# A fused attention and expert kernel: another order on the DMA-issuing engine, and the first expert block's loads and first product moved ahead

## The reference, cut to what matters

```python
def reference(x, ctx, ...):        # x: (2, 1024, 256), ctx: (2, 154, 256)
    x = x + xattn(layernorm(x), ctx, Wq, bq, Wkv, bkv, Wo, bo)
    return x + ffn(layernorm(x), Wg, bg, W1, b1, W2, b2)
# xattn: 16 heads of 16, scores * 1/4 - slope[h] * |k - q - (Nk - Nq)|, softmax over 154 keys,
#        weighted values, output product
# ffn:   gate = softmax(x @ Wg + bg) over 8 experts; the best two, weights made to sum to 1;
#        out = sum over e of (gelu(x @ W1[e] + b1[e]) @ W2[e] + b2[e]) * weight[e]
#        W1[e]: (256, 1024), W2[e]: (1024, 256)
```

## Time and profile before

| | us |
|---|---|
| median of 3 runs | 430.56 |
| lowest, highest | 430.1, 745.77 |
| profiled execution, its time | 427.04 |
| profiled execution, its span | 425.1 |
| PE busy in the span | 383.0 (90%) |
| DVE, ACT, POOL busy | 317.0, 217.8, 186.3 |
| mean granted clock of PE | 0.971 of full |

### The profile page before, as it was taken

One profiled execution on the slowest core, in us unless ns is written; L12 is line 12 of the kernel. 1 busy time (PEld: TensorE's weight loads), 2 busy tenths in 40 slices (PEclk: granted clock), 3 DMA queues, 4 the chain that ended last, 5 costly groups with the idle time before them and its releaser, 6 DMA issues.

```text
span 425.1 us, 15171 instructions
## 1 busy us (share of the span) xinstructions
PE 383.0 (90%) x4834; PEld 300.9 (71%) x4834; DVE 317.0 (75%) x989; ACT 217.8 (51%) x587; POOL 186.3 (44%) x273
## 2 busy tenths in 40 slices
PE   4669999997988999889999999999999999999960
PEld 3547777765766778677777777776778777777740
DVE  6476999997987888834789789776687777777760
ACT  2345778875766766635474344444443444444420
POOL 3300268885766666444454223333133333333341
PEclk9996999999999999969999999999999999999995
DMA  7659768676677964165234553333432333333210
GB/s 277 134 117 277 215 198 239 208 226 206 212 221 215 277 199 149 53 158 156 64 40 84 111 90 47 53 50 47 54 44 39 46 45 46 45 53 47 28 15 0
DMA packets 73441, 50.88 MB, mean 120 GB/s; under 512 B 48400, under 2 KB 67472, under 8 KB 73232
## 3 DMA queue, kind: packets, MB, share of 16 engines
q1 hardware_dynamic: 66168, 41.44, 36.6%
q0 software_dynamic: 7152, 8.47, 12.0%
q10 hardware_dynamic: 48, 0.01, 0.0%
HBM read 28.52 MB, written 17.37 MB: 108 GB/s over the span
## 4 chain that ended last, share of the span: by engine, by line
PE 45%; DMA 2%; DVE 2%; issue 2%; POOL 1%; ACT 1%; ACTq 0%; POOLq 0%; DVEq 0%
PE ps L1256 44%; DMA out<-stage,row_id 2%; DVE area L1171 1%; DVE area L1169 0%; ACT area L800 0%; POOL out L620 0%; POOL xlist L596 0%; ACT L810 0%; DVE st L966 0%; PE ps L1394 0%; DVE stage L1200 0%; DVE stage L1197 0%; DVE xn L847 0%; ACTq L800 0%; DVE stage L1204 0%
## 5 line engine op out<-in xcount | busy, mean ns | idle before, releaser
L1256 PEld LDWEIGHTS ps<-stage,wts 128*128 x1872 | 130.8, 98 | 40.1 <-issue 1.6
L1256 PE MATMUL ps<-stage,wts 128*128 128x128 f16 x1872 | 155.0, 219 | 1.0 <-issue 1.0
L1256 PE MATMUL ps<-wts,area 128*128 x624 | 150.3, 327 | 0.0
L800 ACT ACTIVATE area<-ps,late 128x128 f32<-128x128 f32 x312 | 89.0, 369 | 114.4 <-PE ps L1256 114.4
L620 POOL DMA_INDIRECT out<-stage,row_id x39 | 68.5, 1755 | 130.2 <-DMA out<-stage,row_id 77.2
L1256 PE MATMUL ps<-area 128*128 128x128 f16 (+5 forms) x784 | 63.1, 230 | 10.1 <-DMA area<-qd 7.6
L1169 DVE TENSOR_SCALAR area<-area 128x512 f16<-128x512 f32 x78 | 33.9, 435 | 41.9 <-ACT area L800 39.9
L1256 PEld LDWEIGHTS ps<-area 128*128 128x128 f16 (+1 forms) x784 | 47.4, 104 | 21.6 <-issue 7.5
L917 DVE TENSOR_REDUCE mx<-ps 128x3 f32<-128x462 f32 (+1 forms) x96 | 53.2, 575 | 9.9 <-PE ps L1256 9.8
L1171 DVE SCALAR_TENSOR_TENSOR area<-area 128x512 f16<-128x512 f32 x78 | 54.8, 703 | 2.7
L663 ACT ACTIVATE area<-ps 128x512 f32<-128x512 f32 x80 | 46.5, 600 | 11.7 <-PE ps L1256 11.6
(11 more groups left out here) (131 smaller groups left out, 414.9 us busy)
## 6 DMA issues: line engine op xcount, KB each, us to landing
stage<-in_w SPq DMA_DIRECT2D x32, 512.0 KB, 4.4
area<-qd SPq DMA_DIRECT2D x16, 256.0 KB, 3.7
qd<-wts SPq DMA_DIRECT2D x48, 64.0 KB, 2.1
area<-in_x SPq DMA_DIRECT2D x16, 128.0 KB, 3.3
out<-area SPq DMA_DIRECT2D x16, 128.0 KB
xlist<-pad_rows SPq DMA_DIRECT2D x15, 130.0 KB, 3.5
area<-nbT SPq DMA_DIRECT2D x64, 1.0 KB
area<-in_b SPq DMA_DIRECT2D x1, 1024.0 KB, 5.8
```

Source lines behind the costliest of these rows:

```text
L800: last = nc.scalar.activation(h32[par][:, c * P:(c + 1) * P], h_ps[par][m][:, f * P:(f + 1) * P], ACT.Gelu_apprx_tanh, bias=b1T[:, ds(numb ...
L1256: return nc.tensor.matmul(out_, lhsT, rhs, start=start, stop=stop, skip_group_check=skip)
```

## The change

- `spent` moves from staging places 0 and 1 to places 2 and 3; the last two units, 30 and 31, go to places 0 and 1 (`place_of`, `use_of`), and every wait on a place's count follows.
- SP: in a turn, the store is that of tile i-1 instead of i-2 and stands behind the weights; the constant's piece and the padding rows stand ahead of the weights; `move_m` is last. The four first `load_block`s stand ahead of turn 15 (which issues only the loads of units 30 and 31), and wait for units 26 and 27 instead of 28 and 29.
- PE: `experts` and its register loads stand ahead of turn 15; the four parts of `up(0)` stand behind turn 15 and ahead of `output_turned(15)`. In turns 14 and 15 `transposed(mt, 2)` stands ahead of `second_turned` instead of behind `output_turned`.

```diff
-        spent = stage[:, 0:2, :].rearrange("p s k -> p (s k)")
+        spent = stage[:, 2:4, :].rearrange("p s k -> p (s k)")
+        def place_of(u):
+            return u % NSTAGE if u < UNITS - 2 else u - (UNITS - 2)
+        def use_of(u):
+            return u // NSTAGE if u < UNITS - 2 else UNITS // NSTAGE
 ...  SP, turn(i)
                 if i + 3 < NT:
                     read_q(i + 3)
-                if b2 is not None:
-                    store(b2)
                 if 2 <= i < NT - 6:
                     load_x(i + 6)
                 if f2 is not None:
                     write_q(f2)
-                for u in weight_units(i + 1):
-                    load_w(u)
-                if sc is not None:
-                    move_m(sc)
                 if i in KINK_TURNS:
 ...
+                for u in weight_units(i + 1):
+                    load_w(u)
+                if b1 is not None and i < NT - 1:
+                    store(b1)
+                if sc is not None:
+                    move_m(sc)
-            for i in range(NT):
-                turn(i)
+            for i in range(NT - 1):
+                turn(i)
             sp.wait_ge(s.scat0, 16 * T1)
             sp.wait_ge(s.scat1, 16 * T1)
-            sp.wait_ge(s.w_lo0, UNITS // NSTAGE)
-            sp.wait_ge(s.w_lo1, UNITS // NSTAGE)
+            for u in (UNITS - 6, UNITS - 5):
+                sp.wait_ge(S[f"w_lo{place_of(u)}"], use_of(u) + 1)
             sp.wait_ge(s.sched_done, 2)
             for t in range(4):
                 load_block(t)
+            turn(NT - 1)
 ...  PE, turn(i)
+                if sc is None:
+                    transposed(mt, 2)
                 if b2 is not None:
                     second_turned(b2)
                 if b1 is not None:
 ...
                 if sc is not None:
                     scores(sc, 2)
-                if mt is not None:
                     transposed(mt, 2)
 ...  PE, after the turns
-            for i in range(NT):
+            for i in range(NT - 1):
                 turn(i)
-            for n in range(NSTAGE):
-                pe.wait_ge(S[f"w_lo{n}"], (UNITS - 2 - n + NSTAGE - 1) // NSTAGE)
             e = masked(experts(pe, 0))
+            turn(NT - 1)
+            for n in range(NSTAGE):
+                pe.wait_ge(S[f"w_lo{n}"], (UNITS - 2 - n + NSTAGE - 1) // NSTAGE)
+            w1e = weights(e[0])[:, 0:2, :]
+            for f in range(4):
+                up(0, f, w1e)
             output_turned(NT - 1)
             second_turned(NT - 2)
 ...  then the loop over k, with up() for k > 0 only
```

More of the change, by code:

```diff
@@ L335, in unit_place @@
             return wts[:, e, lo, n * 1024:(n + 1) * 1024].rearrange("p (c k) -> p c k", c=4)
+        def place_of(u):
+            return u % NSTAGE if u < UNITS - 2 else u - (UNITS - 2)
+        def use_of(u):
+            return u // NSTAGE if u < UNITS - 2 else UNITS // NSTAGE
         def staged(u):
-            return stage[:, u % NSTAGE, :].rearrange("p (c k) -> p c k", c=4)
+            return stage[:, place_of(u), :].rearrange("p (c k) -> p c k", c=4)
         def experts(eng, phase):
@@ L379, in load_w @@
             def load_w(u):
-                e, second, n, place = u // 4, u % 4 // 2, u % 2, u % NSTAGE
-                wait(sp, S[f"w_lo{place}"], u // NSTAGE)
+                e, second, n, place = u // 4, u % 4 // 2, u % 2, place_of(u)
+                wait(sp, S[f"w_lo{place}"], use_of(u))
                 if second:
@@ L645, in split_w_hi @@
             def split_w_hi(u):
-                act.wait_ge(S[f"w_stage{u % NSTAGE}"], 16 * (u // NSTAGE + 1))
+                act.wait_ge(S[f"w_stage{place_of(u)}"], 16 * (use_of(u) + 1))
                 if u == UNITS - 4:
@@ L902, in split_w_lo @@
                 dve.scalar_tensor_tensor(out=unit_place(u, 1), in0=staged(u), scalar=SW, in1=unit_place(u, 0),
-                                         op0=ALU.mult, op1=ALU.subtract).then_inc(S[f"w_lo{u % NSTAGE}"], 1)
+                                         op0=ALU.mult, op1=ALU.subtract).then_inc(S[f"w_lo{place_of(u)}"], 1)
             def value(n):
@@ L1586, in _ @@
                 if k == 2 * (K1 - T1 + 1) + 3:
-                    for n in range(NSTAGE):
-                        pe.wait_ge(S[f"w_lo{n}"], UNITS // NSTAGE)
+                    for u in (UNITS - 2, UNITS - 1):
+                        pe.wait_ge(S[f"w_lo{place_of(u)}"], use_of(u) + 1)
                 ahead, here = k < 2 * NBLK, k >= 3 and k not in (2 * NBLK - 2, 2 * NBLK - 1)
-                if ahead:
+                if ahead and k > 0:
                     w1e = weights(e[k // 2])[:, 0:2, :]
```

## The result

| | before | changed |
|---|---|---|
| median of the runs, us | 430.52 | 425.01 |
| profiled execution: its time, its span | 427.04, 425.1 | 424.89, 422.9 |
| mean granted clock of PE | 0.971 | 0.98 |

The ratio is 0.9897, 95% interval 0.9852 to 0.9942: 1.0% faster. In microseconds that is 4.4, by the interval 2.5 to 6.4, where 10.0 were forecast. (The ratio compares the fast runs of both kernels and is not that of the medians, which lie 5.5 us apart.) The time lies within the range, but it is not the forecast's case, and the experiments show that it isn't one case at all: in two later sets of runs, on other chips, the same change is 0.9 and 1.2% slower.

A forecast was written before the change was run, and what follows sets the result against it. It took SP, waiting for a store's landing, to set the pace from about turn 5, not PE. Gains of 7.0 (SP's order) and 3.0 (turn 15), 10.0 us, took 430.56 to 420.6; range 418.8 to 427.3.

The forecast's parts named there:

- the term of 7.0 us: Attention turns 6 to 11: moving SP's store behind the weights shortens its wait, winning 7.0 us of PE's idle time.
- this part removes most of the 7.89 us: Turns 6 to 11: the store's move removes most of PE's 7.89 us idle; at most 7.9, at least about 3.5.
- Constant and padding ahead of the weights: 1.0 us later weights relative to `write_q`, 3 us earlier through the wait removed: covered: SP's order in a turn: the weights' 1.0 us delay is hidden by the 3 us wait removed, so no cost.
- 9.7 "at worst": SP's cycle in attention turns: landing 5.6 plus 4.1 us to the next store, 0.65 over PE's turn.
- rival 4: Attention turns: store landing over 6.5 us takes SP's cycle past 10.6; with 8 us landing, 436.6 us; chance 0.06.
- signs named for this part: SP's store wait under 1.5 us a turn, `read_q` within 5.3 us of turn's beginning, turns 6 to 9 9.05 to 9.3.
- The clock in turn 15: PE's turn 15: less idle time keeps the full clock, so the turn ends at 189.5 instead of 192.55, 3.0 us gained.
- A PE turn needs 9.05: Attention turns: PE's work takes 9.05 us a turn, against SP's cycle of 10.58, so SP sets the pace.
- The base: Whole kernel: gains counted in a 427.04 us profile, the median's 3.5 us difference carried along, starting from 430.56.
- Rival 2: Attention turns: SP stays behind, half of turns 6 to 11's idle time stays; 424.1 us, chance 0.14.
- Rival 1: Turn 15: the clock falls anyway, leaving 0.4 us of that gain; 423.2 us, chance 0.19.
- rival 3: SP held by something else, such as saturated DMA engines, and turn 15 begins late: 0 to 2 us, 429; chance 0.06.

The follow-up runs named there:

- e1: The kernel before, unchanged, run and profiled again: 431.07 us.
- e3: The kernel before with only SP's order in a turn changed as in the change: ratio 0.996 to the kernel before.
- e15: The kernel before with all of the change except SP's order in a turn, run again: 421.98 us, ratio 0.9971 to the kernel before.
- e14: The changed kernel with constant and padding put back behind `move_m`: 416.0 us, ratio 0.9834 to the kernel before.
- e16: The changed kernel, unchanged, run again: 427.1 us, ratio 1.009 to the kernel before.
- the front part: The change without SP's order in a turn: staging places, early `load_block`s, `experts`, `up(0)`, `transposed(mt, 2)`; alone 0.9952 and 0.9971 of the kernel before in two sets.
- e9: The kernel before, unchanged, profiled a third time: ratio 1.0021.
- e4: The changed kernel with SP's order in a turn as before: ratio 0.9952 to the kernel before.
- e8: The changed kernel with every second matmul of `mix` left out, which changes the values: ratio 1.0027 to the kernel before.
- e13: The front part with SP's old order, but `load_x` behind `write_q`, still ahead of the weights: 415.32 us, ratio 0.981 to the kernel before.

## Why the prediction was wrong

**Two steps of the term of 7.0 us failed, one in each case.**

**Where signals are late, as in the changed profile: "this part removes most of the 7.89 us".** That idle time was counted in an execution without late signals, whose turns take 9.05 us when SP keeps up. In the seven profiles with late signals every turn from 3 to 11 takes 9.5 us or more, and in e1, the unchanged kernel, the engines' waits for SP's transfers are 0.5 us in all, while its turns 3 to 10 take 82.2 us. So there was next to nothing for SP's order to win: by itself it gave 1.7 us (e3, by its interval 0.3 to 3.2), not 7.0.

**Where signals are in time, as in the profile of before: "Constant and padding ahead of the weights: 1.0 us later weights relative to `write_q`, 3 us earlier through the wait removed: covered".** Its cover was the wait taken away, and the wait didn't go. On one chip, the store's move gives 6.0 us (e15 to e14), and this edit takes 11.1 (e14 to e16). In the sum both stood as +7.0; together they are -5.1.

**The store behind the weights, 7.0 us.** The mechanism was right: SP's landing sets its cycle, the cycle the lag, the lag the waits. The landing was nearly right as well: 5.6 estimated, 6.0 to 6.2 measured. That agrees with the Trainium skill, "DMA: Bandwidth & Descriptors", "Queues, rings and completion order", that each DMA engine takes one issuer's descriptors in ring order: the store behind two weight units lands at 6.0 instead of 3.6. The other half of that sum was the 4.1 us from landing to next store; it is 4.5 in e16, since the weights' issue takes up to 2.03 us instead of 1.05 (4.1 in the changed profile). 6.2 and 4.5 make 10.7, the old cycle. I had worked out 9.7 "at worst", and then took the value for a landing that is short because SP waits for the residual. That case hardly came up (in the changed profile SP's store waits for the residual twice, 0.7 us in all), for it needs SP to be ahead, which is what was to be shown. The bound of rival 4, a landing over 6.5 us, was missed by 0.3 on the mean and passed in single turns (up to 7.3). Of the signs named for this part, `read_q` does stay within 5.2 us of the turn's beginning in the changed profile, but the wait for the store is 2.8 us a turn and not under 1.5, and turns 6 to 9 take 9.7 to 11.0 us and not 9.05 to 9.3.

**The clock in turn 15, and the front part, 3.0 us.** The clock held, as forecast, and the parts came out within 0.3 us. But the fall that was priced belonged to one execution. From turn 14's start to `second_turned(15)` the first profile of before took 39.0 us, e9 36.1 and e1 37.3; with the front part it is 35.6 and 35.9. So this part is worth 0.5 us where signals are in time and 1.3 where they are late; the runs, with wide intervals, give 1.2 (e15) and 2.1 (e4). That the changed profile is 3.1 us shorter here than the first of before, as forecast, is owed to that one fall.

**"A PE turn needs 9.05".** The number was right and the owner wrong: it is DVE's 8.5 and a wait for POOL of 0.45 (e8). Nothing in the sum hung on it.

**The base.** The forecast carried the 3.5 us between the profiled execution and the median along as noise. Most likely they are the late signals: the profile that the rows come from has none, and the runs that it was scaled to, 430.1 to 430.6, lie among the times of the sets that have them (426.5 to 436.5) and above all of the others (420.4 to 427.9). No trace of those runs is there to show it. That the median of 425.01 came out 4.4 us from the forecast and inside the range is thus no support for its sum.

**The rivals.** Rival 2 (SP stays behind) is what happened where signals are in time, at a price that turns its sign: nothing of the 7.9 us is won. By its own number, 424.1, it would pass for right, but that is luck. Rival 1's fall didn't come, and rival 3's full DMA engines are out: e14 runs them at a share of 0.83 and no engine but SP waits for a transfer of SP's. The better order was near: e13 and e14 are 1.9 and 1.7% faster than the kernel before, and 2.8 and 2.6% faster than the change (e16).

## What to carry to other kernels

When a wait can't be removed, put issues that nobody is late for under it, and keep everything else off the stretch between its end and the next start of what it waits for; write that cycle down as landing plus open part, for each order, before choosing one. A DMA moved ahead of a critical load is priced twice, by its issue and by the load's later landing, and by who stands behind the waiting engine. Before a clock fall or an idle piece of one profile is put into a sum, see it in a second profile of the same kernel, on another chip if there is one.

## What the runs showed of the hardware

- The same kernel has two sets of timings, each seen on other chips: in three sets of runs an engine saw PE's signals 0.3 to 1.4 us late in 22 to 31 places, on the others never. The kernel before takes 428.6 to 431.2 us with them and 423.4 to 424.2 without, and the order of two kernels can turn about. The traces with late signals also hold some 6,800 semaphore records instead of 7,550. What makes them late stays open.
- The granted clock after nearly the same idle piece (1.39, 1.40 and 1.43 us) fell once and held twice. Between turns 3 and 15 falls lasted 3.4 or 6.8 us.
